# Message matmuls set singly between other matmuls on PE, and a new order of steps on VectorE, in a graph-network layer

## The reference

```python
edge_index = jnp.stack([src, dst])
row, col = (edge_index[0], edge_index[1])
msg = jnp.concatenate([src_node_features[col], edge_attr], axis=1)
h = jax.nn.relu(msg @ W1a.T + b1a)
h = h @ W1b.T + b1b
sums = jax.ops.segment_sum(h, row, num_segments=n_nodes)
counts = jax.ops.segment_sum(jnp.ones((h.shape[0],), h.dtype), row, num_segments=n_nodes)
agg = sums / jnp.maximum(counts, 1.0)[:, None]
z = jax.nn.relu(jnp.concatenate([src_node_features, agg], axis=1) @ W2a.T + b2a)
z = z @ W2b.T + b2b
out = jnp.concatenate([z, src_node_features], axis=1) @ Wr.T + br
x = layernorm(x + out)
```

## Time and profile before

| what | value |
|---|---|
| median of 3 runs | 1813.52 us (1808.44 to 1814.13) |
| the profiled execution | 1807.23 us, span 1805.6 us |
| main loop, first to last HH matmul | 55.4 to 1463.6 us |
| mean granted TensorE clock | 0.963 of full |
| PE, VectorE, GpSimd, ScalarE busy | 91%, 78%, 58%, 50% of the span |

### The profile page before, as it was taken

The page is one execution under the profiler, slowest core; times in us unless marked ns, Lnnn a source line. Parts: engine busy times, 40 slices in busy tenths (PEclk is TensorE's granted clock), DMA queues, the critical chain, the costliest instruction groups (busy, mean ns, idle before and its releaser), DMA issues.

```text
span 1805.6 us, 40992 instructions
## 1 busy us (share of the span) xinstructions
PE 1639.8 (91%) x13455; PEld 1341.6 (74%) x13455; DVE 1404.7 (78%) x3936; ACT 905.8 (50%) x1733; POOL 1044.8 (58%) x880
## 2 busy tenths in 40 slices
PE   7899999999999999999999999999999957888787
PEld 6677777777777777777777777777777747777676
DVE  5788888888888888888888888888887745666665
ACT  2365656566565665656666565665656640011101
POOL 2376767677675776757667576775766751112210
PEclk9899999999999999999999999999999988889898
DMA  7355555555554555545555455554555658999994
GB/s 226 87 149 141 155 142 155 146 149 155 141 151 129 157 154 142 152 131 156 153 143 154 127 156 143 154 154 127 155 146 154 167 164 351 354 361 362 339 376 165
DMA packets 127789, 326.02 MB, mean 181 GB/s; under 512 B 35617, under 2 KB 68419, under 8 KB 121310
## 3 DMA queue, kind: packets, MB, share of 16 engines
q0 software_dynamic: 46080, 217.15, 37.3%
q1 hardware_dynamic: 80902, 104.09, 22.7%
q10 hardware_dynamic: 600, 2.16, 0.4%
HBM read 203.87 MB, written 119.40 MB: 179 GB/s over the span
## 4 chain that ended last, share of the span: by engine, by line
PE 77%; DMA 9%; DVE 7%; issue 5%; ACT 1%; POOL 0%; POOLq 0%; DVEq 0%; ACTq 0%
PE MS L492 19%; PE HH L482 19%; PE PA L505 13%; PE PBk L505 12%; DMA gbuf<-region,idx 8%; PE PA L618 5%; PE CK L539 2%; PE RK L565 2%; PE RK L567 2%; DVE OH L1032 1%; DVE M L850 1%; PE RK L577 1%; DVE Z L834 1%; DVE pos L856 0%; POOL region L1109 0%
## 5 line engine op out<-in xcount | busy, mean ns | idle before, releaser
L1109 POOL DMA_INDIRECT region<-stg,dest x806 | 968.1, 1201 | 465.9 <-ACT stg L703 283.9
L482 PE MATMUL HH<-eab,pw 128*128 128x512 f32 x806 | 438.0, 626 | 1.6 <-ACT hT L681 1.6
L850 DVE TENSOR_SCALAR M<-pos_of,pos 128x384 bf16<-128x384 int16 x1612 | 427.1, 314 | 0.1
L492 PE MATMUL MS<-W,hT 128*128 128x64 f32 x3224 | 392.7, 276 | 0.0
L492 PEld LDWEIGHTS MS<-W,hT 128*128 128x128 f32 x3224 | 382.7, 195 | 0.0
L703 ACT ACTIVATE stg<-PA 120x585 bf16<-120x585 f32 x403 | 266.4, 661 | 153.6 <-PE PA L505 153.5
L681 ACT ACTIVATE hT<-HH 128x512 f32<-128x512 f32 x403 | 240.6, 597 | 198.1 <-PE HH L482 198.1
L505 PEld LDWEIGHTS PA<-Z,M 128*128 128x128 bf16 x2418 | 215.1, 97 | 166.1 <-issue 158.0
L505 PE MATMUL PA<-Z,M 128*128 128x195 bf16 x2418 | 290.1, 255 | 38.6 <-issue 34.9
L834 DVE TENSOR_TENSOR Z<-MS,Z 128x512 f32<-128x512 f32 x202 | 139.2, 689 | 196.3 <-ACT Z L692 196.3
L505 PE MATMUL PBk<-Z,M 128*128 128x195 bf16 x2418 | 288.1, 254 | 0.0
(11 more groups left out here) (183 smaller groups left out, 1309.3 us busy)
## 6 DMA issues: line engine op xcount, KB each, us to landing
eab<-in_ea SPq DMA_DIRECT2D x201, 256.0 KB
kb<-keyd SPq DMA_DIRECT2D x201, 128.0 KB
pw<-ptab SPq DMA_DIRECT2D x403, 32.0 KB
region<-stg,dest POOLq DMA_INDIRECT x806
ptab<-OH SPq DMA_DIRECT2D x10, 256.0 KB, 5.0
eab<-in_xt SPq DMA_DIRECT2D x12, 130.0 KB
eab<-in_xt SPq DMA_DIRECT2D x12, 128.0 KB, 8.9
out_y<-kb SPq DMA_DIRECT2D x12, 128.0 KB, 3.6
```

The source lines that it names most:

```text
L482: e.matmul(HH[:, :], pw[:, q % 4, :], eab[:, c % NB, at_q:at_q + GE], start=True, stop=True).then_inc(s_h, 1)
L492: last = e.matmul(MS[:, o:o + D], hT[:, q % 2, 128 * j:128 * j + 128], W[:, W_1B:W_1B + D], start=True, stop=True)
L850: last = e.tensor_scalar(M[:, q % 2, t, :, :], pos_of[:, :, :], pos[:, q % 16, t:t + 1], None, ALU.is_equal)
L1109: e.indirect_dma_start(region, bass.IndirectOffsetOnAxis(ap=dest[:, g:g + 1], axis=0), stw[:, g % NS, :], None).then_inc(s_sc[g % NS], 16)
```

## The change

The message matmuls leave their place behind the second permutation. Those of the even quad go into `permute(2m-2, ...)`, two in each half. Those of the odd quad go into `rank(2m+1)`, each ahead of one of its matmuls. On VectorE, `ranks(2m-1)` comes first in the turn, then all four tiles of places 2m-2, and only then rest and low. `destinations` comes right behind `positions`. `chain_places` is cut in two, and the longer part, `chain_runs`, goes behind places 2m-1, as does `index`. The chain's steps go from 10, 9, 8, 7 to 12, 11, 10, 7 ahead, and `LEAD` from 42 to 44 to match, so the loops run one turn more before the first quad.

```diff
-LEAD = 42
+LEAD = 44
...
+                    def message(q, j):
+                        if j == 0:
+                            if q >= 2 and q % 2 == 0:
+                                e.wait_ge(s_r, q // 2)
                             e.wait_ge(s_relu, q + 1)
...
+                        o = D * (4 * (q % 2) + j)
+                        ins = e.matmul(MS[:, o:o + D], hT[:, q % 2, 128 * j:128 * j + 128],
+                                       W[:, W_1B:W_1B + D], start=True, stop=True)
+                        if j == 3 and (q % 2 or q == NQ - 1):
+                            ins.then_inc(s_msg, 1)
...
+                                if beside is not None and (j, t) in ((0, 1), (2, 0)):
+                                    message(beside, 2 * h + j // 2)
...
+                        if beside is not None:
+                            message(beside, 0)
+                        q = i + 42
...
-                        b = block_at(i, 9)
+                        if beside is not None:
+                            message(beside, 1)
+                        b = block_at(i, 11)
...
+                        if beside is not None:
+                            message(beside, 2)
+                        if 0 <= q < NQ:
                             last = e.matmul(RK[:, 0:4 * CL], sel[:, k:k + 1].to_broadcast([128, 128]),
...
+                        if beside is not None:
+                            message(beside, 3)
...
-                            permute(2 * m - 2, 0)
-                            permute(2 * m - 2, 1)
-                        if 0 <= m < NP:
-                            message(m)
-                        rank(2 * m + 1)
+                            permute(2 * m - 2, 0, even)
+                            permute(2 * m - 2, 1, even)
+                        elif even is not None:
+                            for j in range(4):
+                                message(even, j)
+                        rank(2 * m + 1, odd)
...
+                    def chain_runs(b):
+                        after_link()
                         link(e.tensor_tensor_scan(run_in[:, :], oneg[:, :], kc[:, :], 0.0, ALU.mult, ALU.add))
...
-                        for i in (2 * m + LEAD, 2 * m + LEAD + 1):
-                            if i % BQ == 0 and i < NQ:
-                                index(i // BQ)
+                        ranks(2 * m - 1)
                         if 0 <= m - 1 < NP:
+                            places(2 * m - 2, 0)
+                            places(2 * m - 2, 1)
                             rest(m - 1)
                             low(m - 1)
-                            places(2 * m - 2, 0)
-                        ranks(2 * m - 1)
-                        if 0 <= m - 1 < NP:
-                            places(2 * m - 2, 1)
...
+                        for i in (2 * m - 1, 2 * m):
+                            if block_at(i, 10) is not None:
+                                chain_runs(block_at(i, 10))
+                        for i in (2 * m + LEAD, 2 * m + LEAD + 1):
+                            if i % BQ == 0 and i < NQ:
+                                index(i // BQ)
```

More of the change, by code:

```diff
@@ L379, in pe_ranks @@
         def pe_ranks(i):
-            return (0 <= i + 40 < NQ or 0 <= i + 5 < NQ or 0 <= i + 4 < NQ or block_at(i, 9) is not None
-                    or block_at(i, 8) is not None or block_at(i, 7) is not None or i in (TABLES + 1, TABLES + 2))
+            return (0 <= i + 42 < NQ or 0 <= i + 5 < NQ or 0 <= i + 4 < NQ or block_at(i, 11) is not None
+                    or block_at(i, 10) is not None or block_at(i, 7) is not None or i in (TABLES + 1, TABLES + 2))
         def dve_ranks(i):
-            return (0 <= i + 5 < NQ or block_at(i, 10) is not None or block_at(i, 9) is not None
-                    or block_at(i, 8) is not None or block_at(i, 7) is not None
+            return (0 <= i + 5 < NQ or block_at(i, 12) is not None or block_at(i, 11) is not None
+                    or block_at(i, 10) is not None or block_at(i, 7) is not None
                     or (0 <= i + 4 < NQ and ((i + 4) % 4 == 3 or i + 4 == NQ - 1))
@@ L483, in hidden, with permute @@
                                  start=True, stop=True).then_inc(s_h, 1)
-                    def message(m):
-                        if m >= 1:
-                            e.wait_ge(s_r, m)
-                        for q in range(2 * m, 2 * m + of_pair(m)):
+                    def message(q, j):
+                        if j == 0:
+                            if q >= 2 and q % 2 == 0:
+                                e.wait_ge(s_r, q // 2)
                             e.wait_ge(s_relu, q + 1)
-                            for j in range(4):
-                                o = D * (4 * (q % 2) + j)
-                                last = e.matmul(MS[:, o:o + D], hT[:, q % 2, 128 * j:128 * j + 128],
-                                                W[:, W_1B:W_1B + D], start=True, stop=True)
-                        last.then_inc(s_msg, 1)
-                    def permute(q, h):
+                        o = D * (4 * (q % 2) + j)
[3 more added lines that the diff above has]
+                            ins.then_inc(s_msg, 1)
+                    def permute(q, h, beside=None):
                         P = (PA, PBk)[h]
@@ L508, in permute, with rank @@
                                                 start=t == 0, stop=t == 1)
-                        last.then_inc((s_pA, s_pB)[h], 1)
-                    def rank(i):
+                                if (j, t) == (R - 1, 1):
+                                    last.then_inc((s_pA, s_pB)[h], 1)
+                                if beside is not None and (j, t) in ((0, 1), (2, 0)):
+                                    message(beside, 2 * h + j // 2)
+                    def rank(i, beside=None):
                         if not pe_ranks(i):
+                            for j in range(4 if beside is not None else 0):
+                                message(beside, j)
                             return
@@ L549, in rank @@
                                                     start=t == 0, stop=t == 1)
-                        b = block_at(i, 8)
+                        b = block_at(i, 10)
                         if b is not None:
@@ L601, in _ @@
                         rank(2 * m)
+                        even = 2 * m if 0 <= 2 * m < NQ else None
+                        odd = 2 * m + 1 if 0 <= 2 * m + 1 < NQ else None
                         if 0 <= 2 * m - 2 < NQ:
-                            permute(2 * m - 2, 0)
-                            permute(2 * m - 2, 1)
-                        if 0 <= m < NP:
-                            message(m)
-                        rank(2 * m + 1)
+                            permute(2 * m - 2, 0, even)
[4 more added lines that the diff above has]
+                        rank(2 * m + 1, odd)
                     def gather_sum(c):
@@ L977, in ranks @@
                             positions(i + 5)
-                        if block_at(i, 10) is not None:
-                            chain_copy(block_at(i, 10))
-                        if block_at(i, 9) is not None:
-                            chain_counts(block_at(i, 9))
-                        if block_at(i, 8) is not None:
-                            chain_places(block_at(i, 8))
+                        if 0 <= i + 4 < NQ and ((i + 4) % 4 == 3 or i + 4 == NQ - 1):
+                            destinations(i + 4)
+                        if block_at(i, 12) is not None:
+                            chain_copy(block_at(i, 12))
+                        if block_at(i, 11) is not None:
+                            chain_counts(block_at(i, 11))
+                        if block_at(i, 10) is not None:
+                            chain_places(block_at(i, 10))
                         if block_at(i, 7) is not None:
                             chain_steps(block_at(i, 7))
-                        if 0 <= i + 4 < NQ and ((i + 4) % 4 == 3 or i + 4 == NQ - 1):
-                            destinations(i + 4)
                         if i == TABLES + 1:
```

7 lines of the change are left out of this document (3 added, 4 removed).

## The result

The changed kernel takes 1722.01 us in the median of 4 runs (1713.41 to 1732.64). The kernel before takes 1811.54 us in 4 runs beside it (1808.44 to 1814.13). The ratio is 0.951 with a 95% interval of 0.945 to 0.957, so the change saves about 89 us. The profiled execution takes 1719.57 us, with a span of 1718.0 against 1805.6. The same kernel was run again on another occasion and took 1720.32 us in 6 runs.

A forecast was written before the change was run, and what follows sets the result against it. PE was taken as the bound, with a loop through ScalarE and VectorE adding waits. A block falls from 107.6 to 100.2 us, 7.4 for each of 13 blocks: 1807.2 - 95 = 1712, predicted 1710, range 1684 to 1755.

The forecast's parts named there:

- the ordinary turn: Main-loop turn without index or chain: 6.19 us in the mean after the change, against 6.743 before.
- the four tiles 0.9: VectorE's four M tiles, ahead of rest and low: 0.9 us in the sum of 2.97 to 3.0 up to low.
- the 0.35 for `destinations`: VectorE, every second turn: destinations add 0.35 us ahead of low, making 3.3, so low is 0.07 late.
- Eight edges at 0.035 us: PE's single messages behind bf16 matmuls: eight edges instead of one, seven more at 0.035 save 0.25 us a turn.
- bounds of 0 and 0.64 a turn: PE's message edges: either none saves anything, or each hides the whole 0.092 beside it, 7 x 0.09 = 0.64 us.
- waits of 0.50 and 0.10: PE's waits before the second permutation in the longer and shorter turn, in us; forecast to shrink to 0.07 and 0.
- The chain at 4.3 us a block: VectorE's index and chain delay PE: 4.3 us over ordinary turns for each block, where before it was 3.1.
- its 15 us: Time in the loop where PE runs slow under a lowered clock: 15 us, left unchanged; 15 more or less was possible.
- Loads hide nothing: Rival on PE's message weight loads: only VectorE's order counts, 56 us saved, 1751 us; chance 0.07.
- The switch between number formats costs PE: Rival: 14 more changes between bf16 and float32 on PE at 0.06 us each, 38 us slower, 1845; chance 0.04.
- GpSimd becomes the bound: Rival: four scatters take 6.0 us a turn, OC prolongs two, turn near 6.45, time 1750 us; chance 0.18.
- PE doesn't follow: Rival: the order changes, but something unseen, such as ScalarE, holds the turn at 6.74; time within 0.3%; chance 0.03.

The follow-up runs named there:

- the pairs: The changed kernel with the message matmuls in pairs, four runs of two instead of eight single ones: 1731.78 us, ratio 0.954 against the kernel before.

## Why the prediction was right, point by point

- **The step that was mis-sized: the ordinary turn.** The forecast was 6.16 and 6.2 us, 6.19 in the mean. Measured are 6.17 for one kind and 6.20 or 6.42 for the other. The order held to the hundredth wherever no scatter came in between: `low` is 0.07 late with `destinations` by the sum, and the turn is 0.04 longer. The term that failed is "the four tiles 0.9" and the 0.35 for `destinations`. Both were taken from single rows of VectorE, without a look at what GpSimd does beside them: together they measured 1.28 instead of 1.08 from `dest` to `rest` where a scatter falls badly. 45 turns in the profiled execution lie between 6.3 and 6.5, and 45 x 0.22 = 10 us, about the miss of turns 4 to 196 (forecast 192 x 7.4 / 15.5 = 92, measured 192 x (7.016 - 6.590) = 82). The kernel with `dest` moved and the one without scatters midway show it.
- **Eight edges at 0.035 us.** Right: 6.41, 6.31, 6.17 for one, four and eight runs. The prediction's bounds of 0 and 0.64 a turn were not needed. The Trainium skill, "TensorE: Matmul & The Clock Gate", on packing, lists a load as overlapping only with another row group, though it also speaks of a background weight buffer there. The trace differs from the list: the message's load starts at 505.53, under a full-height permutation matmul, and two permutation matmuls and the message behind them take 0.19 + 0.18 = 0.37 with full-height weights, 0.03 less than 2 x 0.092 + 0.218.
- **What sets the turn of before.** Half right. The prediction called PE the bound and let the loop through VectorE add its waits of 0.50 and 0.10. But taking 0.23 us of PE's work away alone shortens no turn: the loop alone sets it. The sum didn't suffer, as the change does both things at once.
- **The chain at 4.3 us a block.** Right in size: one block has turns of 8.01, 6.78, 7.44 and 6.56 where four ordinary ones would be 24.8 to 25, which is about 4. The longest single wait is 2.2 us, where 2 to 2.9 was forecast. And there is not one such wait in each block: six waits of 1.75 to 2.21 us stand in the loop, for 13 blocks, and the others are under 1.3. The kernel before has six too, of 1.77 and 2.31. It was foreseen that `chain_runs` only moves; that it could be spread, for 38 us (1704 to 1666), was not seen.
- **The clock.** I left its 15 us where they were. In the profiled execution the clock falls five times in the loop, behind waits of 1.75, 2.21, 1.75, 1.75 and 1.27 us; in the other profiled execution of the changed kernel three times, with the same waits; before it was four times. With spread waits it falls once or not at all. The runs of the changed kernel differ by 19 us, and the mean clock goes with them: a run with a span of 1711.7 us has 0.968 and one with 1731.0 has 0.957. My range left room for 15 us each way, which this spread used.
- **The start and the end.** The first four turns cost 87.0 - 56.7 = 30.3 us against 27.9, which is 2.4 more, where the forecast counted some 1.9 less: a miss of 4. The first hidden matmul comes 1.3 later, as forecast. The second phase takes 335.6 instead of 342.0 in the two profiled executions. Another execution of the changed kernel has 345.8, with a shorter loop (1317.2 instead of 1325.7), so this part varies by 10 us from run to run whatever the kernel. The clock goes with it: the second phase has it at 1.2 GHz for 67 us in the execution with 335.6, for 90 in the one with 342.0 and for 94 in the one with 345.8. So the 6.4 us are luck of the execution and not the change's.
- **The sum.** Loop 96 - 10 for the stretched turns - 4 for the first four gives 82 (measured 1408.2 - 1325.7 = 82.5). With 6.4 from the second phase and 1.3 lost at the start it is 87.6, the 87.7 measured. Without the luck of the second phase the saving would have been 81, against the 95 of the sum. The 1710 itself leaned low: it was taken from the profiled execution, and 95 us off the 1811.54 of the median would have been 1717.
- **The rivals.** "Loads hide nothing" is refuted by the pairs. "The switch between number formats costs PE" is refuted by the 6.17. "GpSimd becomes the bound" did not happen in this order (1138 ns), where eight scatters take 8 x (1.14 + 0.30) = 11.5 of the 12.4 to 12.6 us of two turns, but in the order with the ranks behind `low` it held up turns. Of its trigger only half was named: the tiles catch the scatter, OC prolongs it. "PE doesn't follow" is refuted by the turns of 6.17.

## What to carry to other kernels

Before work is taken from the busiest engine, find out whether a turn is set by its work or by a loop of waits through the others: here one half of a change gave nothing alone and 30 us once the other half had opened the loop. Work that comes once in many turns should be paid out in pieces smaller than the slack of a turn, since one long wait costs itself and may cost the clock as well. Where two engines get in each other's way, look at which instruction starts first, and move the one nobody waits for.

## What the runs showed of the hardware that was not expected

- A scatter by indirect DMA that starts inside a row of bf16 `tensor_scalar` tiles lasts until 0.87 us past the end of the row and of an OC in it or right behind it: 1.72 us in a row of four, 2.63 with seven tiles to come, 2.64 in a row of eight. One that started 0.64 ahead of a row took 0.99. The other way round, a scatter that starts 0.06 to 0.10 us behind `dest` holds VectorE up for 0.2 us.
- Waits of 1.3 to 2.2 us in a loop that is otherwise busy are at times followed by a stretch at 1.2 GHz: 23 matmuls in 5 us where 44 stood before. Of eleven waits over 1.2 us in the changed kernel's loop five were followed by one in one execution and three in another.
- A float32 message matmul of 64 columns costs 0.218 in a run and 0.18 behind a bf16 matmul, so part of a full-height weight load does hide under the matmul ahead of it.
